# A six-layer graph-attention stack on one core: the join's sum moved ahead of layer 5's normalise, the low halves ahead of the row minima in two of five slots, and one unit's exponentials split by graph

## The reference

```python
# layer 0: 8 heads of 32
q, k, v = x @ Wq + bq, x @ Wk + bk, x @ Wv + bv
attn = softmax(where(adj == 0, -inf, q @ k.T / sqrt(32)))      # per head
x = layernorm((attn @ v) @ Wo + bo + x) * gamma + beta
# layer 1: one head of 256
w = softmax(where(adj == 0, -inf, (x @ Wq) @ (x @ Wk).T / 16))
x = layernorm(x + (w @ (x @ Wv)) @ Wo + bo) * gamma + beta
# layers 2 to 5: one head of 128, projected values
attn = softmax(where(adj == 0, -1e10, (x @ Wq.T + bq) @ (x @ Wk.T + bk).T / sqrt(128)))
x = layernorm(x + (attn @ x) @ Wc.T) * gamma + beta
```

## Time and profile before

| | |
|---|---|
| runs, median (lowest to highest) | 2340.16 us (2338.4 to 2341.12), 3 runs |
| profiled execution, its own time | 2338.19 us |
| its span, first to last instruction | 2336.4 us |
| granted PE clock, mean | 0.994 |
| busy: PE, DVE, ACT, POOL | 97%, 76%, 69%, 77% |
| `normalise` on DVE (L1007) | 728 instructions, mean 453 ns |

### The profile page before, as it was taken

The page is one execution under the profiler, slowest core; times in us unless marked ns, Lnnn a source line. Parts: engine busy times, 40 slices in busy tenths (PEclk is TensorE's granted clock), DMA queues, the critical chain, the costliest instruction groups (busy, mean ns, idle before and its releaser), DMA issues.

```text
span 2336.4 us, 59698 instructions
## 1 busy us (share of the span) xinstructions
PE 2257.7 (97%) x20624; PEld 2132.9 (91%) x20624; DVE 1771.6 (76%) x7736; ACT 1614.4 (69%) x5515; POOL 1787.6 (77%) x2397
## 2 busy tenths in 40 slices
PE   6899999999999999999999999999999999999986
PEld 5799999999999999999999999999999999999985
DVE  4777877877877877777777777777778778777776
ACT  5667767767767767767767767767677677677653
POOL 3368878878878878878788788788788788788762
PEclk9999999999999999999999999999999999999998
DMA  4000110110110110010010100100100100000000
GB/s 157 20 24 24 31 29 24 31 29 24 31 29 24 30 30 24 27 33 22 29 31 24 28 29 26 29 28 27 28 29 26 29 27 28 29 25 26 11 15 14
DMA packets 38747, 68.78 MB, mean 29 GB/s; under 512 B 4400, under 2 KB 12848, under 8 KB 37936
## 3 DMA queue, kind: packets, MB, share of 16 engines
q1 hardware_dynamic: 38448, 64.97, 9.2%
HBM read 48.18 MB, written 16.78 MB: 28 GB/s over the span
## 4 chain that ended last, share of the span: by engine, by line
PE 78%; DVE 9%; ACT 8%; issue 2%; POOL 2%; DMA 0%; POOLq 0%; SPq 0%; DVEq 0%
PE value_bank L464 17%; PE qk_bank L456 16%; PE context_bank L619 9%; PE unit_bank L464 8%; PE unit_bank L456 7%; PE score_bank L603 5%; PE qk_bank L569 5%; ACT probs L740 5%; PE unit_bank L523 5%; PE unit_bank L535 3%; PE score_bank L600 2%; DVE scores L919 2%; PE score_bank L610 2%; DVE xT_lo L948 2%; DVE scores L954 1%
## 5 line engine op out<-in xcount | busy, mean ns | idle before, releaser
L1190 POOL TENSOR_TENSOR x<-y,rows 128x512 f32<-128x512 f32 x304 | 390.3, 1284 | 188.5 <-DVE y L1007 188.5
L740 ACT ACTIVATE probs<-scores,negmax 128x128 f32<-128x128 f32 x1024 | 400.8, 400 | 88.9 <-DVE negmax L919 88.9
L1007 DVE TENSOR_SCALAR y<-y,mv,rstd 128x256 f32<-128x256 f32 x728 | 299.4, 453 | 175.7 <-POOL rstd L1174 175.5
L456 PE MATMUL qk_bank<-xT_hi,w_lo 128*128 128x256 f32 x1280 | 414.9, 324 | 17.0 <-DVE xT_lo L948 13.0
L1198 POOL TENSOR_TENSOR x<-x,rows 128x512 f32<-128x512 f32 x304 | 392.5, 1291 | 19.1
L762 ACT CAST xT_hi<-qk_bank 128x512 fp32r<-128x512 f32 x257 | 150.1, 584 | 355.0 <-PE qk_bank L569 354.9
L464 PE MATMUL value_bank<-w_lo,xT_hi 128*128 128x256 f32 x1280 | 393.7, 308 | 0.0
L456 PE MATMUL qk_bank<-xT_lo,w_hi 128*128 128x256 f32 x1280 | 362.5, 283 | 0.0
L456 PE MATMUL qk_bank<-xT_hi,w_hi 128*128 128x256 f32 x1280 | 360.8, 282 | 0.0
L464 PE MATMUL value_bank<-w_hi,xT_lo 128*128 128x256 f32 x1280 | 360.8, 282 | 0.0
L464 PE MATMUL value_bank<-w_hi,xT_hi 128*128 128x256 f32 x1280 | 358.8, 280 | 0.0
(11 more groups left out here) (98 smaller groups left out, 6532.7 us busy)
## 6 DMA issues: line engine op xcount, KB each, us to landing
x0T<-xT_in SPq DMA_DIRECT2D x64, 256.0 KB, 3.0
x<-x_in SPq DMA_DIRECT2D x64, 256.0 KB, 3.1
out<-x_out SPq DMA_DIRECT2D x64, 256.0 KB, 2.3
adj<-adj_in SPq DMA_DIRECT2D x64, 128.0 KB, 2.2
late_weights<-w_in SPq DMA_DIRECT2D x2, 1024.0 KB, 7.3
rows<-rows_in SPq DMA_DIRECT2D x1, 1792.0 KB, 11.6
probs0T<-w_in SPq DMA_DIRECT2D x4, 256.0 KB, 4.1
x<-w_in SPq DMA_DIRECT2D x1, 1024.0 KB, 13.1
```

What stands on the lines that cost most here:

```text
L456: mm = pe.matmul(psum[:, n * G * N:(n + 1) * G * N], split(w, name, kd, at, at + P), flat(xT_half[:, kd]), start=kd == 0 and w is w_lo, st ...
L740: e = act.activation(probs0[:, j, g, quad], scores0[:, j, g, quad], ACT.Exp, scale=-1.0, bias=negmax0[:, j, g, quad:quad + 1], accum_out=t ...
L1007: m = dve.tensor_scalar(y[:, r, g], y[:, r, g], mv[:, r, g, 0:1], rstd[:, r, g:g + 1], ALU.subtract, ALU.mult)
L1190: pool.tensor_tensor(result(norm), y[:, NORM_AT[norm] % YS], row_of_each(f"gamma{layer}"), ALU.mult).then_inc(zg_ready, 1)
```

## The change

Three edits, all of order.

1. In slot 3, DVE does `add_residual` and `statistics` of layer 0's norm (the join's sum) before it normalises layer 5's item, and POOL does `find_rstd(group)` before `scale(item)` of layer 5.
2. In slots 4 and 0 (`urgent`), DVE does `split_lo`, and in slot 4 `normalise(group)` too, before `row_max`.
3. `exp0` takes a list of graphs. Of unit 0, graph 0's two exponentials stay in slot 4. Graph 1's two move to slot 0, behind `split_hi`, and the semaphore is raised there.

```diff
 # ACT
-            def exp0(group, j):
+            def exp0(group, j, graphs=range(G)):
                 act.wait_ge(negmax0_ready, after_unit(group, j))
-                for g in range(G):
+                for g in graphs:
...
-                e.then_inc(exp0_ready, 1)
+                if g == G - 1:
+                    e.then_inc(exp0_ready, 1)
...
             for i in LOOP_SLOTS:
                 if item(i):
                     split_hi(i)
+                if (group := due(i, 5)) is not None and item(i - 1):
+                    exp0(group, 0, [1])
...
                 if (group := due(i, 6)) is not None:
-                    exp0(group, 0)
+
+                    exp0(group, 0, [0] if item(i) else range(G))
 # DVE
             for i in LOOP_SLOTS:
-                if item(i - 1):
+
+                urgent = due(i, 1) is not None or due(i, 0) is not None
+                if item(i - 1) and not urgent:
                     row_max(i - 1)
                 if item(i):
                     split_lo(i)
                 if (group := due(i, 1)) is not None:
                     finish_or_normalise(("group", group))
+                if item(i - 1) and urgent:
+                    row_max(i - 1)
...
-                if item(i - 2):
-                    finish_or_normalise(("item", i - 2))
                 if (group := due(i, 2)) is not None:
                     add_residual(("group", group))
                     statistics(("group", group))
+                if item(i - 2):
+                    finish_or_normalise(("item", i - 2))
 # POOL
                 if item(i - 1):
                     keep_valid(i - 1)
+                if (group := due(i, 2)) is not None:
+                    find_rstd(("group", group))
                 if item(i - 2):
                     scale(("item", i - 2))
...
                 if (group := due(i, 2)) is not None:
-                    find_rstd(("group", group))
                     scale(("group", group))
                     shift(("group", group))
```

## The result

The changed kernel takes 2434.33 us (median of 5 runs, 2433.78 to 2438.16), the kernel before 2340.16 (median of 5 as well, 2338.26 to 2341.12): a ratio of 1.0407, 95% interval 1.0393 to 1.0422. The forecast was 2435, with a range from 2366 to 2458. The profiled execution has a span of 2432.3 us (2336.4 before), with the granted clock at 0.995 (0.994), so PE's clock has no part in it.

A forecast was written before the change was run, and what follows sets the result against it. PE, busy 97%, was taken as the bound, so only added PE waits matter. Slot 1's `project_qk` 1.58 late in 60 turns gave 95 us: 2338.2 becomes 2433, plus 2.0 for the median 2435 us; range 2366 to 2458.

The forecast's parts named there:

- The start of the relay: Slot 3 into 4: join's sum starts 0.71 earlier; `normalise(group)` starts at 1120.54, beside POOL's `scale` of layer 5.
- Slot 4 and T: `normalise(group)` is held by POOL's `scale`; T, the end of slot 4's item `normalise`, moves from 1126.01 to 1126.60.
- `score` of slot 0: PE, start of slot 0: starts 0.10 earlier, at 1125.07, because `move_probsT` on ACT ends 0.10 earlier.
- Slot 0: `split_lo` first makes `row_max` 1.20 late; `normalise` then meets POOL's `shift`, and slot 1's `project_qk` is 1.58 late.
- Where PE waits: PE, every slot 1: one wait of more than 1 us for `xT_lo`, each turn some 1.6 us longer.
- The sum: Whole kernel: 60 turns x 1.58 = 95 us lost, profiled execution 2433, median 2435 us; chance 0.48.
- One meeting only: Rival: DVE's `normalise` is held by a long POOL instruction in only one of slots 4 and 0; 2407, chance 0.14.
- no meeting: Rival: overlap of `normalise` with POOL costs nothing; slot 1's `project_qk` about 0.61 late, 37 us, 2377; chance 0.10.
- The floor of the slower cases: Least loss if slower: `split_lo`'s 0.61 ahead of slot 0's `row_max`, 60 x 0.61 = 37 us, 2377.
- Faster: Rival: the end of slot 4 counts, `score` of slot 0 up to 0.66 earlier, 40 us won, 2300; chance 0.11.
- The `pow` blocks as well: Rival: POOL's `pow` also holds up DVE's `normalise`, beyond the two forecast meetings; 2451, chance 0.14.

The follow-up runs named there:

- join_alone: Kernel before with edit 1 alone (join's sum ahead of layer 5's normalise on DVE): 2355.75 us against 2337.25, ratio 1.008.
- small_scale: Changed kernel with POOL's `scale` of layer 5 cut to one column of each graph, order unchanged: 2400.87 us, ratio 1.0274 to the kernel before.
- exp_alone: Kernel before with edit 3 alone (unit 0's exponentials split by graph between slots 4 and 0): 2333.00 us against 2337.25, ratio 0.9981.
- slot0_undone: Changed kernel, but slot 0 takes `row_max` ahead of `split_lo` again: 2376.23 us against 2337.25 for the kernel before, ratio 1.0165.
- small_shift: Changed kernel with POOL's `shift` of layer 5 cut to one column of each graph: 2407.90 us, ratio 1.0305 to the kernel before.
- small_both: Changed kernel with POOL's `scale` and `shift` of layer 5 both cut to one column of each graph: 2368.41 us, ratio 1.0135 to the kernel before.

## Why the prediction was right, and where it was off

**The start of the relay.** Right within 0.1. Set back by 45.97, the aggregate ends at 1118.96 (forecast 1118.94), `scale` of layer 5 starts at 1120.12 (1120.02), and `normalise(group)` starts at 1120.51 (1120.54) and ends at 1121.85 (1121.78). Its pair takes 1.34, where these times gave 1.24. The prediction says 1.0 from statistics to rstd but reckons with 1.10; the trace has 1.10 in slot 4 and 1.18 here, beside the `normalise`, which is the 0.1 that `scale` is late. join_alone shows that this edit alone loses, 18.5 us against 16 expected.

**Slot 4 and T.** Right: T is 1126.64, forecast 1126.60. The price of the meeting there was argued from rows of slot 0 and is now shown. small_scale takes POOL's long instruction away, the pair falls from 1.34 to 0.73, and 33.5 us come back.

**`score` of slot 0.** Off by a little: forecast 0.10 earlier, it is 0.01 earlier (1171.13 - 45.97 = 1125.16 against 1125.17). As forecast it hangs on `move_probsT`: it starts 0.14 after that ends (1170.63 + 0.36 = 1170.99), the same distance as before. But `move_probsT` is itself 0.01 earlier and not 0.10, since the pair of slot 4 and all that follows it on DVE was 0.07 later than I had it. The transposes ahead of `score`, which start at 1124.64 instead of 1124.32 after a wait of 0.24 for `shift`, would have left little more: in exp_alone, where `move_probsT` ends early, `score` follows them after 0.49, here after 0.52.

**Slot 0.** Right: `softmax` 1127.70 (forecast 1126.46 + 1.20 = 1127.66), the reciprocal 1131.12 (1129.88 + 1.20 = 1131.08), POOL's multiplies 1131.38 (1131.35), the pair from 1132.09 to 1134.00 (1132.05 to 1133.96), `project_qk` of slot 1 at 1135.07 (1135.05). From `softmax` to `split_hi` ACT has no gap, 1179.24 - 1173.67 = 5.57, as before. slot0_undone shows that the 0.61 ahead of `row_max`, with the meeting that it brings about, is worth 55 to 58 of the 94 us. small_shift shows that the meeting alone is worth 26.4, where 0.47 x 60 = 28 were expected.

**Where PE waits.** The step that failed: I put the whole loss into one wait of more than 1 us for `xT_lo` in slot 1. The loss is there, but in two waits, 0.38 for the moved values in slot 0 and 0.54 for `xT_lo` in slot 1, with smaller ones beside them. By starts, `project_v` of slot 0 is 0.75 late (1175.56 - 45.97 = 1129.59 against 1128.84) and `project_qk` of slot 1 then 1.60; that is why slot 0 grows by 0.98 and slot 1 by 0.62. The line of the kernel before:

```profile
1128.84 0.36 PE L464 MATMUL value_bank<-w_lo,xT_hi 128*128 128x256 f32 x1
```

`move_v` hangs on the same chain on ACT, and I didn't follow it. The sum is untouched, since it was taken at slot 1's `project_qk`, to which both belong.

**The sum.** 60 x 1.58 = 95 was forecast. The medians give 94.2, the spans 2432.3 - 2336.4 = 95.9, and the turn 36.85 - 35.22 = 1.63. At 60 turns that would be 98, so a turn a little dearer than forecast and some 2 us won outside the full turns cancel. The agreement within 1 us is luck; that within 5 us is not.

**The rivals.** *One meeting only* and *no meeting* did not happen, but could be built: small_scale and small_shift are 62 and 69 us above their runs of before (67 forecast), small_both 29.8 (37). The floor of the slower cases was some 7 us too high. By the turn small_both loses 0.55 where 0.61 was forecast, which is half of it; why is open. *Faster* falls with exp_alone: the gain at the end of slot 4 is real in that kernel (0.37), and 0.29 of it is gone at the end of slot 0.

*The `pow` blocks as well* did not happen. `normalise` of layer 5 takes 0.70 (1164.84 to 1165.54) while the `pow` has begun at 1165.38. But my reason for it, the small operand, is not shown by this, since the `pow` was the later of the two, by about 0.2. It took 0.73 instead of 0.71, and the add ahead of it 0.28, where slot 4's takes 0.22. The Trainium skill ("SBUF — State Buffer", Who interferes with whom) lets the one that issues first keep the shared pair. So its rule, read by the order of issue, agrees in that the `normalise` was not held, and I had read it without asking which of the two comes first. The add shows that recorded starts alone don't settle it: it began 0.12 before the second half (1165.02 against 1165.14), and that half took 0.41, as alone. A `pow` that begins before a `normalise` half beside it is in none of the traces.

## What to carry to other kernels

When engines work in a fixed order, look first for a stretch in which one of them has no gap, and price each edit by when that stretch begins. Here more than half of the loss came through the late start of one `softmax` in slot 0 and the meeting that followed it. An edit that makes a result earlier can push a long GpSimd instruction beside a VectorE instruction that used to run alone, and the pair then ends with the long one. So compare the start times of both engines before and after, not only their order on each: beside the semaphores, such a meeting is a second link between the engines.

## What the runs showed of the hardware

In the trace of the changed kernel, 120 halves of `normalise` (0.41 us alone) met a POOL instruction of 1.3 us, and each ended 0.15 to 0.16 us after it; 57 met a multiply of 0.6 us and ended 0.15 after it too. That makes the pairs of 1.34 and 1.91, where 0.74 is usual. In 119 of the 120 POOL had begun first, by 0.07 to 0.40 us; in one the half had begun 0.08 before, and was held all the same. An add on 2 columns that began 0.12 us before a half and ended within its first 0.16 us cost it nothing. Where DVE began first, a POOL instruction on 2 columns lost 0.02 to 0.06 us.
